# VectorE's order in a steady step of graph attention: low part of p, addition of adj, then the running maximum of the step before

## The reference

```python
def _L0_gnn_ref(x, spatial_encoding, edge_encoding, Wq, bq, Wk, bk, Wv, bv):
    q = x @ Wq.T + bq
    k = x @ Wk.T + bk
    v = x @ Wv.T + bv
    scale = 1.0 / jnp.sqrt(jnp.asarray(q.shape[-1], q.dtype))
    a = q @ k.T * scale + spatial_encoding + edge_encoding
    attn = jax.nn.softmax(a, axis=-1)
    return attn @ v
h = jnp.maximum(_layernorm(x, axis=-1), 0.0)
x = x + _L0_gnn_ref(h, adj, adj, Wq, bq, Wk, bk, Wv, bv)
```

## Time and profile before

| | |
|---|---|
| median of 3 runs | 805.36 us (805.24 to 805.49) |
| the profiled execution | 805.12 us, its span 803.3 us |
| TensorE busy | 798.9 us (99%), granted clock 1.0 |
| VectorE busy | 560.0 us (70%) |
| ScalarE busy | 356.0 us (44%) |
| GpSimd busy | 412.3 us (51%) |
| chain that ended last | TensorE 99% of it: L431 51%, L555 to L557 15% each |

### The profile page before, as it was taken

One profiled execution on the slowest core, in us unless ns is written; L12 is line 12 of the kernel. 1 busy time (PEld: TensorE's weight loads), 2 busy tenths in 40 slices (PEclk: granted clock), 3 DMA queues, 4 the chain that ended last, 5 costly groups with the idle time before them and its releaser, 6 DMA issues.

```text
span 803.3 us, 16607 instructions
## 1 busy us (share of the span) xinstructions
PE 798.9 (99%) x6642; PEld 797.1 (99%) x6642; DVE 560.0 (70%) x950; ACT 356.0 (44%) x636; POOL 412.3 (51%) x369
## 2 busy tenths in 40 slices
PE   9999999999999999999999999999999999999998
PEld 8999999999999999999999999999999999999998
DVE  7869667667666766767666766767676676676664
ACT  6764444444444443434344344434434434443375
POOL 4656538092652908256190734719174370926573
PEclk9999999999999999999999999999999999999999
DMA  8522433333332434334333333333333343333300
GB/s 258 207 70 74 118 86 119 93 112 106 99 106 81 137 92 113 93 99 117 81 125 93 124 90 99 110 92 112 98 108 105 93 118 93 106 104 94 93 27 14
DMA packets 46398, 83.57 MB, mean 104 GB/s; under 512 B 5616, under 2 KB 8304, under 8 KB 46320
## 3 DMA queue, kind: packets, MB, share of 16 engines
q1 hardware_dynamic: 45744, 81.71, 34.3%
q10 hardware_dynamic: 576, 0.79, 0.3%
HBM read 78.25 MB, written 4.23 MB: 103 GB/s over the span
## 4 chain that ended last, share of the span: by engine, by line
PE 99%; DVE 0%; issue 0%; POOL 0%; DVEq 0%; POOLq 0%
PE ps L431 51%; PE ps L555 15%; PE ps L556 15%; PE ps L557 15%; PE ps L423 1%; PE ps L408 1%; PE ps L438 0%; PE ps L483 0%; PE ps L519 0%; DVE x_res L832 0%; DVE x_res L821 0%; PE ps L458 0%; DVE p_lo L812 0%; PE ps L530 0%; PE ps L537 0%
## 5 line engine op out<-in xcount | busy, mean ns | idle before, releaser
L431 PE MATMUL ps<-qhl,hT 128*128 128x256 f32 x3060 | 406.2, 283 | 0.0
L431 PEld LDWEIGHTS ps<-qhl,hT 128*128 128x128 f32 x3060 | 382.3, 190 | 0.0
L555 PE MATMUL ps<-v,p_hi 128*128 128x258 f32 x1024 | 290.6, 284 | 0.3 <-DVE p_lo L812 0.3
L556 PE MATMUL ps<-v,p_lo 128*128 128x258 f32 x1024 | 288.9, 282 | 0.0
L557 PE MATMUL ps<-v,p_hi 128*128 128x256 f32 x1024 | 288.2, 281 | 0.0
L699 ACT CAST p_hi<-ps 128x512 fp32r<-128x512 f32 x256 | 150.5, 588 | 262.6 <-PE ps L557 261.0
L398 POOL TENSOR_TENSOR ring_a<-ring_a,m_row 128x512 f32<-128x512 f32 x179 | 226.8, 1313 | 16.0 <-ACT m_row L705 15.3
L767 DVE TENSOR_TENSOR ring_a<-ps,ring_a 128x512 f32<-128x512 f32 x179 | 123.5, 690 | 117.7 <-PE ps L431 116.5
L555 PEld LDWEIGHTS ps<-v,p_hi 128*128 128x128 f32 x1024 | 194.5, 190 | 0.9 <-DVE p_lo L812 0.7
L556 PEld LDWEIGHTS ps<-v,p_lo 128*128 128x128 f32 x1024 | 194.7, 190 | 0.0
L557 PEld LDWEIGHTS ps<-v,p_hi 128*128 128x128 f32 x1024 | 193.4, 189 | 0.0
(11 more groups left out here) (85 smaller groups left out, 338.0 us busy)
## 6 DMA issues: line engine op xcount, KB each, us to landing
ring_a<-in_adj SPq DMA_DIRECT2D x179, 256.0 KB, 2.7
ring_b<-in_adj SPq DMA_DIRECT2D x77, 256.0 KB, 2.7
x_res<-in_x SPq DMA_DIRECT2D x16, 256.0 KB, 3.0
out<-x_res SPq DMA_DIRECT2D x15, 256.0 KB, 2.0
x_pair<-in_x SPq DMA_DIRECT2D x5, 512.0 KB, 4.2
term_row<-term_spill SPq DMA_DIRECT2D x14, 128.0 KB, 3.2
x_third<-in_x SPq DMA_DIRECT2D x2, 512.0 KB, 4.7
w_all<-in_w ACTq DMA_DIRECT2D x2, 257.0 KB, 3.7
```

What stands on the lines that cost most here:

```text
L431: last = nc.tensor.matmul(dst, lhs(a, ib), rhs(c, ib), start=(n == 0), stop=(n == 3 * DB - 1))
L555: nc.tensor.matmul(ps[:, at, 0:VW], hi, v[:, n, 0:VW], start=(n == 0), stop=False)
L556: nc.tensor.matmul(ps[:, at, 0:VW], lo, v[:, n, 0:VW], start=False, stop=False)
```

## The change

In each iteration of VectorE's steady loop the low part of p and the addition of adj now come ahead of the running maximum, which is still that of step s - 1. running_max gets a second argument, by which it waits until the addition of step s, now ahead of it, is done. At the end of the last block, where nothing is added any more, the last maximum waits for the one before it by the semaphore s_kept. What finish(), reduce_max(), turn_terms() and q_lo() do is unchanged: finish() stays first, reduce_max() and turn_terms() still follow the maximum and so come behind the addition, q_lo() stays last.

```diff
-            def running_max(s):
+            def running_max(s, added=0):
                 b, u = s // UNITS, s % UNITS
                 if u == 0:
                     return
-                dve.wait_ge(s_add, s + 1)
+                dve.wait_ge(s_add, max(s + 1, added))
                 kept = acc[:, :] if b == 0 else ps[:, A_BANK, :]
                 first = slot(s - 1) if u == 1 else kept
                 to = acc[:, :] if u == UNITS - 1 else kept
                 if b == 0 and u > 1:
                     dve.wait_ge(s_kept, u - 1)
+                if s == STEPS - 1:
+                    dve.wait_ge(s_kept, UNITS - 1)
                 last = nc.vector.tensor_tensor(to, first, slot(s), ALU.max)
-                if b == 0 and u < UNITS - 1:
+                if (b == 0 and u < UNITS - 1) or s == STEPS - 2:
                     last.then_inc(s_kept, 1)
...
                 if s not in HOLD and 0 < due(s) < STEPS and due(s) % UNITS == 0:
                     finish(due(s) // UNITS - 1)
+                if s not in HOLD and 0 <= due(s) + 1 < STEPS:
+                    write_p_lo(due(s) + 1)
+                if s < STEPS:
+                    add_adj(s)
                 if s - 1 < STEPS:
-                    running_max(s - 1)
+                    running_max(s - 1, min(s + 1, STEPS))
                 if u == 1 and b - 1 in TURNED:
                     reduce_max(b - 1)
                 if s == FIRST + 3:
                     turn_terms(1, GROUPS)
-                if s not in HOLD and 0 <= due(s) + 1 < STEPS:
-                    write_p_lo(due(s) + 1)
-                if s < STEPS:
-                    add_adj(s)
                 if u == UNITS // 2 and b + 1 < BLOCKS:
                     q_lo(b + 1)
```

## The result

| | before | after |
|---|---|---|
| median | 805.34 us (805.24 to 805.49, 5 runs) | 818.26 us (817.57 to 819.09, 5 runs) |
| ratio | 1 | 1.0161, 95% interval 1.0150 to 1.0172 |
| profiled execution | 805.12 us, span 803.3 | 818.35 us, span 816.6 |

The change makes the kernel 1.6% slower: 12.9 us by the medians, 13.2 by the profiled executions. The forecast was 817.0, with 811.5 to 820.5. The ratios further down are to the kernel before, timed again beside each experiment (805.13 to 805.27).

What follows compares the result with a forecast made beforehand. TensorE was taken to bound the kernel, busy 798.9 of 803.3 us. 805.12 + 8.3 (block ends) + 2.7 (first block) + 0.8 (last block) = 816.9, stated as 817.0 us, range 811.5 to 820.5.

Steps and rivals of the forecast that it cites:

- both parts are needed: At block ends, finish() is late only with both the exp 2.85 us late and a maximum moved ahead of finish().
- The block ends: In 14 of 16 blocks finish() comes 0.59 us late and TensorE waits for it: 8.3 us, bounds 4.1 to 12.5.
- the one from all-reduce to exp: GpSimd's chain at a block end, from all-reduce to first exp: 11.24 us in the mean, its wait 7.20.
- The gap between maximum and reciprocal: In finish() at a block end: 0.61 us, taken from the trace; by the page's rule about 0.09 more, 818.2 in all.
- The first block: TensorE's turn slips 0.66 us and its spread waits for a later reduce_max: 2.7 us, bounds 2.0 to 3.0.
- later steps have no rest: After the first block's delay of 2.7 us, TensorE has no rest in later steps to take it back.
- The last block: The last maximum and L790 come later, so the turn slips 1.04 us, of which 0.20 was rest: 0.8 us.
- Steady steps: VectorE's loop keeps the same three instructions in the same cyclic order with unchanged gaps: 0 us.
- The pauses weren't given back: Rival: TensorE regains its pauses by running queued products at 0.107 us instead of 0.12; 805.3 us, 4%.
- TensorE's granted clock: Part of the "worse" rival: clock falls behind the 2.05 us pause, costing 7.2 us at 1.2 GHz; 821 to 824, 10%.
- Only the ends cost: Rival: the block ends' chain arrives 0.6 us earlier than reckoned and finish() keeps its time; 808.6 us, 7%.

Runs made afterwards that it cites:

- reduce_max_early: The change, but reduce_max() stands ahead of the low part and the addition of its step, as before the change: 817.56 us (1.0151).
- max17_from_psum: The change, but ScalarE copies step 16's logits to PSUM, so the maximum of step 17 reads one input from SBUF instead of two: 818.84 us, single time.
- row_max_in_psum: Against reduce_max_early: the reduced maximum lies in the running maximum's PSUM bank, so the addition behind it has one SBUF input instead of two: 817.15 us (1.0148).

## Why the prediction was right, point by point

**Direction and cause.** Right. TensorE had no room at one place, finish() at a block's end, and the change makes it late there. The two conditions it named ("both parts are needed") each proved necessary: without the late exp 808.1 us, without the maximum ahead 807.5 or 809.6, with both 818.3.

**The block ends: 8.3 us forecast, 9.6 found.** Loads of TensorE at the start of the products with v, in the kernel before and then after:
```profile
76.22 0.19 PEld L555 LDWEIGHTS ps<-v,p_hi 128*128 128x128 f32 x1
...
739.86 0.19 PEld L555 LDWEIGHTS ps<-v,p_hi 128*128 128x128 f32 x1
```
```profile
79.22 0.19 PEld L555 LDWEIGHTS ps<-v,p_hi 128*128 128x128 f32 x1
...
752.46 0.19 PEld L555 LDWEIGHTS ps<-v,p_hi 128*128 128x128 f32 x1 [0.66 <-DVE x_res L823]
```
The distance was 3.00 us when the first block's maximum was through and 12.60 at the last finish() ahead of the tail: 9.6 over 14 blocks, 0.69 each where 0.59 was reckoned. In this block end every gap used in the sum came out to 0.02: 1.45, 0.56, 0.63, 0.61, 0.72, 0.60. The term that was off is the one from all-reduce to exp, 11.34 us in the mean of 14 blocks after (11.03 to 11.78) against 11.24 before. Its wait inside the all-reduce grew from 7.20 to 7.31:
```profile
POOL m_row L385 <- issue: 102.3, 14, 7.7
```
That wait differs from execution to execution: 101.5 to 103.4 us in total in the variants, and 100.8 before, the least of all twelve traces. So the row that the forecast took it from was a short one. TensorE now feels it 14 times: with 101.5, 102.3, 102.9 and 103.0 us of it, in reduce_max_early, the change, max17_from_psum and row_max_in_psum, its waits for finish() were 8.2, 9.0, 9.5 and 10.1. That fits with runs of the kernel after that lie 1.5 us apart, and those of before 0.25. Why it varies stays open.

**The gap between maximum and reciprocal.** 0.60 us behind a maximum of 0.70, so it was right to take the gap from the row, not from the rule; at 0.70 the sum would have been nearer by accident. The section of the Trainium skill that the prediction names ("VectorE: DVE Perf Modes", "The DRAIN you can't avoid") also says that an instruction that isn't "held" (bound to wait until all earlier ones have finished) starts earlier. The 0.60 us here agree with that.

**The first block: 2.7 forecast, 3.0 found.** The turn waited 0.74 and the spread 1.97 (2.05 forecast). 0.09 of the 3.0 stood ahead of the turn already (the load ahead of it starts at 65.73 against 65.64) and are not the change's. Not in the sum were the 0.20 us for an addition, held by a maximum with two inputs in SBUF. The forecast had "later steps have no rest", but not that a moved instruction may meet GpSimd's reads.

**The last block: 0.8 forecast, 0.6 found** (13.2 between the profiled executions less 12.6). The turn waited 0.98 us.

**Steady steps: 0 us.** Right: addition, maximum and low part keep their distances, and with both ends mended and the shared reads removed the new order gives 805.20 us. To about 0.6 us, the cycle by itself is neither better nor worse.

**The rivals.** The pauses weren't given back: the 0.81 us added per block showed in full, and the 0.81 taken out gave back nearly all that the block ends had cost. Behind the pause of 2 us 36 loads took 4.37 us, still 0.12 each. TensorE's granted clock stayed at 1.0 (2.4 GHz) from 69 to 72 us, with the pause, and from 72 to 75, so the pause cost only itself. "Only the ends cost" came true when the chain was cut by 0.81 us: 809.4 against 808.6 forecast for that case.

## What to carry to other kernels

A cyclic reorder that leaves the steady state alone is decided at the seams: list what happens once a block (finish, the last maximum) and ask which neighbour each now stands behind. Where the bottleneck engine has no room, a move that uses up the last 0.1 us is free by itself and so is a delay elsewhere, but together they cost 0.7 us a block; mending either, by putting finish() ahead of one maximum or one maximum a block back in its place, gives most of it back. When VectorE's instructions with two inputs in SBUF are moved, look what GpSimd does at the new time.

## What the runs showed of the hardware

A VectorE tensor_tensor with both inputs in SBUF waited for the GpSimd instruction that was under way, whatever its own size: 1.46 us instead of 0.70 for 512 numbers a partition, 1.09 instead of 0.16 for 2, 1.16 instead of 0.42 for 256. With one input in PSUM it didn't, beside the same GpSimd instruction (0.16 and 0.70). The Trainium skill says so ("SBUF — State Buffer", section "Who interferes with whom": an instruction of VectorE with two inputs in SBUF contends with one of GpSimd that reads SBUF, through the read interface that the two share); the runs agree. Who comes first decides who waits: in the kernel before it was GpSimd's subtraction, 1.84 us instead of 1.31. The all-reduce is different: the maximum of u = 1, with two inputs in SBUF, falls some 4.5 us behind its start (404.80 against 400.33 in the kernel after) and keeps its 0.70 us, so at that point it doesn't hold the port:
```profile
404.80 0.70 DVE L781 TENSOR_TENSOR ps<-ring_a 128x512 f32<-128x512 f32 x1
```
